# Layer norm chunks 1 to 7 turned one per step through the first product's bank, over twelve written-out steps, with the branch on the mask moved ahead

## The chip, the cores and the metric

The kernel runs on one core of one Trainium2 chip. The time is device microseconds (us) of one execution. Before the change three runs gave 430.34 us as median (429.97 to 431.79). The profiled execution took 429.76 us.

## The reference, cut to what matters

The input x has the shape (4, 32, 32, 128). Two blocks follow each other: a Swin block (layer norm, window attention with 16 heads of 8 channels in 64 windows of 64 tokens, projection, a gated MLP) and then a self-attention over 1024 tokens of each image. The change touches only the start of the first block:

```
xn = _layer_norm(x, norm1_g, norm1_b)            # over the 128 channels
xs = roll(xn, (-4, -4)); xw = windows of 8 x 8   # 64 windows, 64 tokens
qkv = xw @ qkv_w.T + qkv_b
q, k = rope2d(q), rope2d(k)
attn = softmax(q * scale @ k.T + attn_mask)      # attn_mask is 0 or -100
out = attn @ v
```

## The kernel before, in words

Five engines run instruction streams written by hand, and meet in semaphores: TensorE (PE), VectorE (DVE), ScalarE (ACT), GpSimd (POOL) and SyncE (SP), which issues transfers. Each works its own stream in order. The 4096 tokens lie in `x_all` as 32 pairs of windows, 128 tokens each. The layer norm takes four pairs at a time: 8 chunks of 512 tokens.

**A chunk of the layer norm** passes five stations: DVE takes the statistics (`ln_stats_of`, lines 800 and 804, four of each), POOL works out 1/sqrt(var + eps) and the shift (`ln_rstd_of`, lines 1041 to 1046), ACT scales the rows into `xn` (`ln_norm_of`, line 945, four instructions), PE transposes them into a PSUM bank (`ln_turn`, line 648, four f32 transposes), ACT copies the bank as its f16 high part (`ln_hi_of`), and DVE takes the rest as its f16 low part (`ln_lo_of`, line 819), which counts `ln_ready` up. Chunk 0 is done ahead of all steps.

**A step n** of the window attention, from -2 to 34, works on several pairs at once. PE's order in it is: the first product, q and k of pair n+2, into bank 4, `QKV_BANK` (lines 668 and 670); the first turn of pair n+1 (line 706, eight transposes, q and k); the scores of pair n (line 678, two mask products, then 687); the turned scores of pair n-1 (lines 678 and 699); the product with v of pair n-3 (line 761); the v product of pair n-1 (668, 670); the second turn of q of pair n (line 706, four transposes). Beside it DVE takes the two rope products from bank 4 (line 855), copies the first turn out (869), takes the low part of v (880), the row maxima of the scores (887) and writes them as two f16 columns (892, 894) that the second turn needs, and at last divides by the row sums (908, 912). ACT writes the q and k rows, the exponential (line 993), the copy of the second turn `q_t`, the high part of v, and the high part of the probabilities `p_hi` (those four from line 931 in the helper `copy`). POOL sums the rope (1064), takes the low part of the probabilities (1072) and those of q and k (1076, 1078). SP issues four transfers from `qk_t` to `k_t` (line 637), and the scores of a pair wait for them.

**Where the chunks stand before the change.** Chunks 1 and 2 are normed ahead of the steps and turned at the end of step -2 and in step -1. Chunks 3 and 4 are turned in step 0, 5 in step 1, 6 and 7 in step 2. They go through the banks of the turned scores and of the product with v (`LN_BANK`), which stand empty until step 3; `LN_BANK_FREE` tells which earlier chunk must be out. Steps -2 to 3 are written out, 4 to 27 are a loop of four steps with six passes, and 28 to 34 are written out.

**The branch on the mask.** PE has the steps from 0 on twice: with three bf16 parts of the mask and with one. The drawn mask needs one. PE reads the flag `mask_any` into a register in step -1, turns pair 0, waits for ACT's copy of the mask (`mask_hi`), and then branches.

Of the kernel before, what the change touches and what calls it, by code (L numbers as in the profile page):

```python
# [20 lines left out]
B, H, W, DIM = 4, 32, 32, 128  # L21
# [21 lines left out]
BUFS = 4  # L43
# [7 lines left out]
def build(nc, t):  # L51
    ctx = ExitStack()
    with ctx:
# [496 lines left out]
        with ExitStack() as st:  # L550
# [40 lines left out]
            def first_steps(body):  # L591
                for n in range(FIRST, 0):
                    body(n, n // 2, n % BUFS)

# [10 lines left out]
            def steps(eng, body, mlp_early):  # L605
                first_steps(body)
                other_steps(eng, body, mlp_early)

            def at_step(n, step):
                return isinstance(n, int) and n == step  # L610

            def valid(n, lag):
# [29 lines left out]
            def _(pe):  # L642
                def ln_turn(c):

                    pe.wait_ge(ln_norm, c + 1)
                    wait(pe, ln_ready, LN_BANK_FREE[c])
                    for k in range(TPC):
                        last = pe.transpose(ps[:, LN_BANK[c], 128 * k:128 * k + 128],
                                            xn[:, c % 4, 128 * k:128 * k + 128], ident[:])
                    last.then_inc(ln_turned, 1)  # L650
# [53 lines left out]
                def turn(out, rows):  # L704
# [3 lines left out]
                    return last  # L708

                def body(n, it, r, parts):  # L710
                    u = r % 2
                    v = 1 - u

                    if valid(n, -2):
                        wait(pe, rope_done, n + 2)

                        pe.wait_ge(ln_ready, (n + 2) // TPC + 1 if isinstance(n, int) and n < LOOP_FROM else CHUNKS)
                        project(qkv_ps[:, 0:2 * DIM], n + 2, slice(0, 2 * DIM)).then_inc(qk_done, 1)
                    if at_step(n, -2):

                        pe.wait_ge(mask_top, 1)
                        pe.matmul(ps[0:1, T1_BANK, 0:1], mask_max[:], ln_const[:, 2, 0:1], start=True,
                                  stop=True).then_inc(mask_summed, 1)
                    if at_step(n, -1):
                        ln_turn(2)

                        pe.wait_ge(mask_known, 1)
                        rest.append(pe.value_load(mask_any[0:1, 0:1].bitcast(mybir.dt.int32)))
                    if valid(n, -1):
# [4 lines left out]
                    if valid(n, 0):  # L734
# [3 lines left out]
                        scores(qk_t[:, u, 0], k_t[:, r], it, parts).then_inc(s_done, 1)  # L738
                    if at_step(n, 0):
                        ln_turn(3)  # L740
                        ln_turn(4)
                    if at_step(n, 1):

                        pe.wait_ge(ln_ready, 5)
                    if at_step(n, 2):
                        ln_turn(6)
                    if valid(n, 1):
# [3 lines left out]
                        scores_turned(k_t[:, (r - 1) % BUFS], q_t2[:, v], it if u else it - 1, parts).then_inc(st_done, 1)  # L751
                    if at_step(n, 1):
                        ln_turn(5)
                    if valid(n, 3):
                        wait(pe, plo_done, n - 2)
                        wait(pe, norm_done, n - 3)
                        pe.wait_ge(ln_ready, CHUNKS)
# [16 lines left out]

                    if at_step(n, -2):
                        ln_turn(1)
                    if at_step(n, 2):
                        ln_turn(7)

                rest = []  # L780
                first_steps(lambda n, it, r: body(n, it, r, 1))
                pe.wait_ge(mask_hi, 1)
                with pe.If(rest[0] > 0):
                    pe.wait_ge(mask_lo, 1)
                    other_steps(pe, lambda n, it, r: body(n, it, r, 3), mlp_pe(pe)[1])
                with pe.If(rest[0] < 1):
                    other_steps(pe, lambda n, it, r: body(n, it, r, 1), mlp_pe(pe)[1])

            @block.vector
            def _(dve):  # L790
# [25 lines left out]
                def ln_lo_of(c):  # L816

                    dve.wait_ge(ln_hi, c + 1)
                    dve.tensor_tensor(xn_all[:, TPC * c:TPC * c + TPC, 1, :],
                                      ps[:, LN_BANK[c], :].rearrange("p (t q) -> p t q", t=TPC),  # L820
                                      xn_all[:, TPC * c:TPC * c + TPC, 0, :], ALU.subtract).then_inc(ln_ready, 1)
# [24 lines left out]
                def body(n, it, r):  # L846
# [14 lines left out]
                    if at_step(n, -1):  # L861
                        ln_lo_of(1)
                        ln_stats_of(3)
                    if at_step(n, 3):
                        ln_lo_of(7)
                    if valid(n, -1):
# [3 lines left out]
                    if at_step(n, -1):  # L870
                        ln_lo_of(2)
                        ln_stats_of(4)
                        ln_stats_of(5)
                        ln_stats_of(6)
                    if valid(n, 2):
# [8 lines left out]
                    if valid(n, 0):  # L884
# [10 lines left out]
                                                 op0=ALU.mult, op1=ALU.subtract).then_inc(mlo_done, 1)  # L895
                    if at_step(n, 0):
                        ln_lo_of(3)
                        ln_lo_of(4)
                        ln_stats_of(7)
                    if at_step(n, 1):  # L900
                        ln_lo_of(5)
                    if at_step(n, 2):
                        ln_lo_of(6)
                    if valid(n, 3):
# [16 lines left out]
            def _(act):  # L921
# [11 lines left out]
                def ln_hi_of(c):  # L933

                    act.wait_ge(ln_turned, c + 1)
                    copy(xn_all[:, TPC * c:TPC * c + TPC, 0, :],
                         ps[:, LN_BANK[c], :].rearrange("p (t q) -> p t q", t=TPC)).then_inc(ln_hi, 1)

# [19 lines left out]
                ln_hi_of(0)  # L958
                ln_norm_of(1)
                ln_norm_of(2)  # L960
                ln_hi_of(1)

                def body(n, it, r):
# [10 lines left out]
                    if at_step(n, -1):  # L974
                        act.wait_ge(mask_loaded, 16)
                        copy(mask16[:, 0], mask_f[:]).then_inc(mask_hi, 1)
                        ln_norm_of(3)
                        ln_norm_of(4)

# [3 lines left out]
                        copy(proj_w16[:, 0, :], proj_ws[:]).then_inc(proj_w_hi, 1)  # L983
                    if at_step(n, 0):
                        ln_hi_of(3)
                        ln_hi_of(4)
                    if at_step(n, 2):
                        ln_hi_of(6)
                    if valid(n, 1):
# [4 lines left out]
                                       ACT.Exp).then_inc(exp_done, 1)  # L994
                    if at_step(n, 1):
                        ln_hi_of(5)
                        ln_norm_of(6)
                    if valid(n, 0):
# [3 lines left out]
                    if valid(n, 1):  # L1002
# [9 lines left out]
                        copy(p_hi[:, v], e_buf[:, v]).then_inc(phi_done, 1)  # L1012
                    if at_step(n, -2):
                        ln_hi_of(2)
                    if at_step(n, 0):
                        ln_norm_of(5)
                    if at_step(n, 1):
                        ln_norm_of(7)
                    if at_step(n, 2):
                        ln_hi_of(7)  # L1020

# [3 lines left out]
            def _(pool):  # L1025
# [31 lines left out]
                def body(n, it, r):  # L1057
# [22 lines left out]
                    if at_step(n, -1):  # L1080
                        ln_rstd_of(3)
                        ln_rstd_of(4)

                        pool.wait_ge(mask_known, 1)
                        with pool.If(pool.value_load(mask_any[0:1, 0:1].bitcast(mybir.dt.int32)) > 0):
# [12 lines left out]
                                .then_inc(mask_lo, 1)  # L1098
                    if at_step(n, 0):
                        ln_rstd_of(5)  # L1100
                        ln_rstd_of(6)
                    if at_step(n, 1):
                        ln_rstd_of(7)

                        pool.wait_ge(proj_w_hi, 1)
# [591 lines left out]
```

## Time and profile before

| what | value |
|---|---|
| median of three runs | 430.34 us (429.97 to 431.79) |
| the profiled execution | 429.76 us, its span 428.0 us |
| busy in the span: PE, DVE, ACT, POOL | 369.4, 306.4, 261.3, 231.6 us |
| of the chain that ended last: PE, DVE, ACT, issue | 59%, 19%, 9%, 5% |
| mean granted TensorE clock | 0.956 |

A busy time is the sum of an engine's instructions; the chain that ended last follows from the last instruction back through what released each one. In it "issue" is time in which the engine waited for nothing that the profile shows. Times are counted from the start of the span.

### The profile page before, as it was taken

How to read it: one execution, taken by the hardware profiler on the slowest of the kernel's cores; microseconds unless marked ns; L12 is line 12 of the kernel's file. 1: busy time of each engine (PE TensorE's matmuls, PEld its weight loads, DVE VectorE, ACT ScalarE, POOL GpSimd, SP SyncE). 2: the span in 40 equal slices, each digit the busy share in tenths (PEclk: the TensorE clock that was granted, in tenths of full speed). 3: DMA queues.
4: the chain of work that ended last, by engine and by line, in shares of the span. 5: the costliest groups of instructions: out<-in, count | busy, mean ns of one | idle time of the engine just before them, and what ended most of it. 6: DMA issues, size and time to landing. Idle time of an engine off the chain costs nothing.

```text
span 428.0 us, 12372 instructions
## 1 busy us (share of the span) xinstructions
PE 369.4 (86%) x4708; PEld 230.2 (54%) x4708; DVE 306.4 (72%) x850; ACT 261.3 (61%) x409; POOL 231.6 (54%) x288
## 2 busy tenths in 40 slices
PE   2567899999999999993999999999449998989794
PEld 0234555656566566572455555554215776767563
DVE  8767788888888888876465655553789787784524
ACT  2768777778777878692434333333407867768572
POOL 6656476777787777767253223310004774857511
PEclk9999999999999999996799999999957999999889
DMA  6701010110001100100000000000100102010101
GB/s 192 252 23 28 14 32 24 31 28 25 25 28 28 30 25 26 32 9 2 0 3 0 2 0 1 2 0 2 51 0 0 26 3 76 2 51 2 41 11 50
DMA packets 15580, 12.52 MB, mean 29 GB/s; under 512 B 3991, under 2 KB 14136, under 8 KB 15416
## 3 DMA queue, kind: packets, MB, share of 16 engines
q1 hardware_dynamic: 14144, 11.42, 9.2%
q10 hardware_dynamic: 1400, 0.61, 0.5%
q8 instruction: 24, 0.39, 0.4%
q14 instruction: 12, 0.10, 0.1%
HBM read 4.68 MB, written 2.10 MB: 16 GB/s over the span
## 4 chain that ended last, share of the span: by engine, by line
PE 59%; DVE 19%; ACT 9%; issue 5%; POOL 4%; DMA 2%; SPq 1%; DVEq 0%; POOLq 0%; ACTq 0%
PE ps L306 8%; PE ps L1324 7%; PE ps L314 6%; PE ps L678 5%; PE ps L706 5%; DVE mx L1460 4%; PE ps L668 3%; PE ps L761 3%; PE ps L1268 3%; PE ps L699 3%; PE ps L687 3%; DVE ob L1498 2%; DVE ps L887 2%; PE ps L670 2%; PE ps L1307 2%
## 5 line engine op out<-in xcount | busy, mean ns | idle before, releaser
L1586 POOL TENSOR_TENSOR el<-e,eh 128x1024 f16<-128x1024 f32 x28 | 59.6, 2132 | 77.7 <-ACT eh L1578 77.5
L1072 POOL TENSOR_TENSOR p_lo<-e_buf,p_hi 128x1024 f16<-128x1024 f32 x32 | 68.3, 2135 | 5.0 <-ACT p_hi L931 3.7
L1571 ACT ACTIVATE e<-ps 128x1024 f32<-128x1024 f32 x32 | 32.7, 1022 | 38.9 <-PE ps L1313 38.5
L306 PE MATMUL ps<-y_t,fc_w 128*128 128x512 f16 x192 | 47.7, 393 | 0.0
L1460 DVE TENSOR_REDUCE mx<-ps 128x1 f32<-128x1024 f32 x32 | 39.0, 1219 | 9.8 <-PE ps L1297 9.4
L1064 POOL TENSOR_TENSOR rot<-ta,tb 128x256 f32<-128x256 f32 x32 | 23.3, 729 | 40.5 <-DVE tb L855 40.4
L1324 PE MATMUL ps<-val,eh 128*128 128x129 f16 x512 | 38.3, 225 | 6.1 <-DVE ob L1498 5.3
L887 DVE TENSOR_REDUCE ps<-ps 128x16 f32<-128x1024 f32 x32 | 39.4, 1232 | 3.1 <-PE ps L687 2.2
L993 ACT ACTIVATE e_buf<-ps 128x1024 f32<-128x1024 f32 x32 | 32.8, 1024 | 14.4 <-PE ps L699 14.3
L678 PE MATMUL ps<-mask,identb 128*128 (+1 forms) x128 | 39.0, 386 | 2.6 <-DMA k_t<-qk_t 2.4
L1324 PEld LDWEIGHTS ps<-val,eh 128*128 128x128 f16 x512 | 32.8, 100 | 14.8 <-issue 8.8
L493 ACT ACTIVATE sg<-ps,fc_bias 128x512 f32<-128x512 f32 x32 | 22.0, 688 | 29.6 <-PE ps L306 26.6
L668 PE MATMUL ps<-qkv_w,xn_all 128*128 128x128 f16 (+1 forms) x192 | 27.4, 252 | 9.3 <-issue 7.7
L314 PE MATMUL ps<-hid,fc_ws 128*128 128x512 f32 x64 | 33.9, 611 | 0.8 <-POOL al L252 0.7
L931 ACT ACTIVATE p_hi<-e_buf 128x1024 f16<-128x1024 f32 x32 | 33.8, 1057 | 0.8
L403 DVE SCALAR_TENSOR_TENSOR hid<-ps,fc_bias,sg 128x512 f32<-128x512 f32 x32 | 24.0, 749 | 14.4 <-ACT sg L493 13.4
L1578 ACT ACTIVATE eh<-e 128x1024 f16<-128x1024 f32 x32 | 33.7, 1054 | 0.7
L306 PEld LDWEIGHTS ps<-y_t,fc_w 128*128 128x128 f16 x192 | 19.1, 101 | 27.8 <-issue 9.3
L706 PE MATMUL ps<-ident,q_rows 128*128 128x128 f16 x256 | 25.8, 224 | 5.0 <-DVE q_rows L894 3.2
L931 ACT ACTIVATE q_t<-ps 128x512 f16<-128x512 f16 x32 | 19.1, 597 | 12.7 <-PE ps L706 12.7
L699 PEld LDWEIGHTS ps<-q_t,k_t 128*64 128x64 f16 x1024 | 18.7, 112 | 13.6 <-issue 13.6
L761 PE MATMUL ps<-v_hi,p_hi 128*128 128x36 f16 x256 | 23.0, 180 | 2.0 <-POOL p_lo L1072 1.9
(148 smaller groups left out, 919.9 us busy)
## 6 DMA issues: line engine op xcount, KB each, us to landing
k_t<-qk_t SPq DMA_DIRECT2D x128, 32.0 KB, 1.8
x_all<-in_x SPq DMA_DIRECT2D x8, 256.0 KB, 5.8
out<-ob SPq DMA_DIRECT2D x8, 192.0 KB, 2.1
mask_f<-in_mask SPq DMA_DIRECT2D x1, 1024.0 KB, 4.8
yr<-xr SPq DMA_DIRECT2D x14, 64.0 KB, 2.0
fc_w<-in_fc_w SPq DMA_DIRECT2D x1, 512.0 KB, 7.1
out<-ob SPq DMA_DIRECT2D x4, 128.0 KB, 1.8
fc_w<-in_fc_w SPq DMA_DIRECT2D x1, 256.0 KB, 6.9
```

The costliest lines, as they stand in the source:

```text
L306: last = pe.matmul(ps[:, bank, :], fc1_w16[:, ws, 128 * block_:128 * block_ + 128], y_t[:, v, ys, :], start=(n == 0), stop=(n == 2))
L314: pe.matmul(ps[:, OUT_BANK, :], fc2_ws[:, k, :], hid[:, k % 2, :], start=(k == 0), stop=False, skip_group_check=True).then_inc(h_used, 1)
L668: pe.matmul(out, xn_all[:, at(i, 1), xs, :].rearrange("p a q -> p (a q)"), qkv_w16[:, ws, cols], start=(n == 0), stop=False, skip_group_ch ...
L678: pe.matmul(ps[:, bank + b, :].rearrange("p (h k) -> p h k", h=8), identb[:], mm, start=(part == 0), stop=False, skip_group_check=True)
L706: last = pe.transpose(out[:, c, :], rows[:, 4 * c:4 * c + 4, :].rearrange("p h r -> p (h r)"), ident16[:])
L761: last = pe.matmul(out, p[:, v, 2 * hp:2 * hp + 2, :].rearrange("p h q -> p (h q)"), w[:, v, hp].rearrange("p e r d -> p (e r d)"), start= ...
L887: dve.tensor_reduce(mx_ps, ps[:, S_BANK:S_BANK + 2, :].rearrange("p b (h k) -> p (b h) k", h=8), AX.X, ALU.max).then_inc(max_done, 1)
L931: return act.activation(out, in_, ACT.Copy)
L1072: pool.tensor_tensor(p_lo[:, u], e_buf[:, u], p_hi[:, u], ALU.subtract).then_inc(plo_done, 1)
L1324: return pe.matmul(pv4[:, j, i, 0:DIM + 1], weights[:, T % H_BUFS, 128 * n:128 * n + 128], val[:, b % 2, part, m, 0:DIM + 1], start=first, ...
L1460: dve.tensor_reduce(mx[:, k:k + 1], two(s_bank(k)), AX.X, ALU.max, negate=True).then_inc(max4_done, 1)
L1586: pool.tensor_tensor(el[:, T % H_BUFS, :], e4[:, T % E_BUFS, :], eh[:, T % H_BUFS, :], ALU.subtract).then_inc(el_done, 1)
```

## The change

Bank 4 now serves all chunks. Steps -2 to 11 are written out, and the loop runs from 12 to 27 in four passes. Chunks 1, 2, 3, 4, 5, 6, 7 are turned in steps 0, 2, 4, 6, 8, 10, 11, each after the scores of that step and ahead of the turned scores. ACT norms a chunk at the end of its step before (chunk 1 in step -1), copies its high part ahead of the exponential; DVE takes the low part after the maxima. The next first product waits for it, as it needs the same bank. The statistics of chunks 3 and 4 stay in step -1, now behind the copy of the first turn, and those of 5, 6, 7 go to steps 1, 3, 5; POOL's part of 3 to 7 goes to steps 1, 3, 5, 7, 9. PE issues the two first products of steps -2 and -1 next to each other, reads the flag, branches, and does the first turn of pair 0 and the wait for the mask's copy behind the branch.

```diff
-            LOOP_FROM, LOOP_TO = 4, PAIRS - 4
-            LN_BANK = (PV_BANK, ST_BANK, ST_BANK + 1, PV_BANK, ST_BANK, PV_BANK, PV_BANK, PV_BANK)
-            LN_BANK_FREE = (0, 0, 0, 1, 2, 4, 6, 7)
+            LOOP_FROM, LOOP_TO = 12, PAIRS - 4
+            LN_STEP = {0: 1, 2: 2, 4: 3, 6: 4, 8: 5, 10: 6, 11: 7}
...
+                def first_product(n):
+                    wait(pe, rope_done, n + 2)
+                    wait(pe, ln_ready, max([1] + [c + 1 for k, c in LN_STEP.items() if k < n])
+                         if isinstance(n, int) else CHUNKS)
+                    project(qkv_ps[:, 0:2 * DIM], n + 2, slice(0, 2 * DIM)).then_inc(qk_done, 1)
...
-                    if at_step(n, 0):
-                        ln_turn(3)
-                        ln_turn(4)
-                    if at_step(n, 1):
-                        pe.wait_ge(ln_ready, 5)
-                    if at_step(n, 2):
-                        ln_turn(6)
+                    if ln_chunk(n):
+                        pe.wait_ge(rope_done, n + 3)
+                        ln_turn(ln_chunk(n))
...
+                first_product(-2)
+                pe.wait_ge(mask_top, 1)
+                pe.matmul(ps[0:1, T1_BANK, 0:1], mask_max[:], ln_const[:, 2, 0:1], ...)
+                first_product(-1)
+                pe.wait_ge(mask_known, 1)
+                rest = pe.value_load(mask_any[0:1, 0:1].bitcast(mybir.dt.int32))
+                def steps_of(parts):
+                    part = lambda n, it, r: body(n, it, r, parts)
+                    part(-1, -1, BUFS - 1)
+                    pe.wait_ge(mask_lo if parts > 1 else mask_hi, 1)
+                    other_steps(pe, part, mlp_pe(pe)[1])
+                with pe.If(rest > 0):
+                    steps_of(3)
+                with pe.If(rest < 1):
+                    steps_of(1)
...   (DVE, after the maxima)
+                    if ln_chunk(n):
+                        ln_lo_of(ln_chunk(n))
+                    for c, step in ((5, 1), (6, 3), (7, 5)):
+                        if at_step(n, step):
+                            ln_stats_of(c)
...   (ACT, ahead of the exponential, and at the end of the step)
+                    if ln_chunk(n):
+                        ln_hi_of(ln_chunk(n))
...
+                    if isinstance(n, int) and n != -1 and ln_chunk(n + 1):
+                        ln_norm_of(ln_chunk(n + 1))
...   (POOL, at the end of the step)
+                    for c, step in ((3, 1), (4, 3), (5, 5), (6, 7), (7, 9)):
+                        if at_step(n, step):
+                            ln_rstd_of(c)
```

## Rows read from the trace of the kernel before

**Rows 1.** Windows: start:end length, then busy (count) per engine, PEclk, DMA share, GB/s.
```profile
14.00:18.00 4.00, 3.46 (x19) 2.07 (x17) 2.58 (x13) 2.75 (x8) 2.32 (x5) 1.00 1.06 371
37.58:44.99 7.41, 5.19 (x72) 3.35 (x73) 3.93 (x10) 7.31 (x17) 3.92 (x6) 1.00 0.07 20
50.23:70.97 20.74, 19.36 (x353) 12.05 (x353) 17.32 (x44) 15.47 (x29) 14.70 (x20) 1.00 0.11 29
70.97:90.53 19.56, 19.14 (x353) 12.05 (x353) 17.13 (x46) 15.76 (x29) 14.56 (x20) 1.00 0.09 26
```

**Rows 2.** Chain that ended last, 15 to 30 us: start, length, what.
```profile
18.59 1.81 ACT mask L931
20.40 4.13 issue
```

**Rows 3.** Timeline of PE around the branch: start, length, instruction, [idle before <-releaser].
```profile
14.26 0.85 PE L668 MATMUL ps<-qkv_w,xn_all 128*128 128x256 f16 x3
17.02 0.61 PE L706 MATMUL ps<-ident,q_rows 128*128 128x128 f16 x4 [0.54 <-POOL k_rows L1078]
24.53 0.80 PE L668 MATMUL ps<-qkv_w,xn_all 128*128 128x256 f16 x3 [6.48 <-issue]
26.42 1.06 PE L678 MATMUL ps<-mask,identb 128*128 128x512 bf16 x2
28.40 1.09 PE L648 MATMUL ps<-ident,xn 128*128 128x128 f32 x8
30.33 0.40 PE L706 MATMUL ps<-ident,q_rows 128*128 128x128 f16 x4 [0.83 <-DVE q_rows L894]
30.56 0.49 PE L668 MATMUL ps<-qkv_w,xn_all 128*128 128x256 f16 x3
```

**Rows 4.** Timeline of PE, first products of steps 2, 3, 4; turn of chunk 7.
```profile
35.80 0.49 PE L668 MATMUL ps<-qkv_w,xn_all 128*128 128x256 f16 x3
...
43.44 0.63 PE L648 MATMUL ps<-ident,xn 128*128 128x128 f32 x4 [1.85 <-DVE xn_all L819]
43.90 0.49 PE L668 MATMUL ps<-qkv_w,xn_all 128*128 128x256 f16 x3
...
50.23 0.50 PE L668 MATMUL ps<-qkv_w,xn_all 128*128 128x256 f16 x3
```

**Rows 5.** Timeline of PE, one loop step and the loop's back edge.
```profile
104.95 0.50 PE L668 MATMUL ps<-qkv_w,xn_all 128*128 128x256 f16 x3
...
107.13 0.61 PE L678 MATMUL ps<-mask,identb 128*128 x2
...
109.40 0.40 PE L706 MATMUL ps<-ident,q_rows 128*128 128x128 f16 x4
110.13 0.28 PE L668 MATMUL ps<-qkv_w,xn_all 128*128 128x256 f16 x1 [0.33 <-issue]
```

**Rows 6.** Timeline of ACT: norm of chunk 7, then the same loop step.
```profile
39.70 1.63 ACT L945 ACTIVATE xn<-x_all,nmr,rstd 128x128 f32<-128x128 f32 x4
...
105.08 0.60 ACT L931 ACTIVATE q_t<-ps 128x512 f16<-128x512 f16 x1 [0.37 <-PE ps L706]
...
106.19 1.06 ACT L931 ACTIVATE p_hi<-e_buf 128x1024 f16<-128x1024 f32 x1
```

**Rows 7.** Timeline of DVE: statistics, a low part, maxima of the loop step.
```profile
31.33 0.86 DVE L800 BATCH_NORM_STATS2 stats<-x_all 128x6 f32<-128x128 f32 x4
...
42.60 0.69 DVE L819 TENSOR_TENSOR xn_all<-ps,xn_all 128x512 f16<-128x512 f32 x1 [1.47 <-ACT xn_all L931]
...
107.59 1.23 DVE L887 TENSOR_REDUCE ps<-ps 128x16 f32<-128x1024 f32 x1
```

**Rows 8.** Chain that ended last, 50 to 57 us: copy, transfer, scores.
```profile
51.76 0.69 DVE qk_t L869
...
54.69 1.84 DMA k_t<-qk_t
56.58 0.60 PE ps L678 x2
```

More of the change, by code:

```diff
@@ L582, in build @@
             FIRST, LAST = -2, PAIRS + 2
-            LOOP_FROM, LOOP_TO = 4, PAIRS - 4
-            LN_BANK = (PV_BANK, ST_BANK, ST_BANK + 1, PV_BANK, ST_BANK, PV_BANK, PV_BANK, PV_BANK)
-            LN_BANK_FREE = (0, 0, 0, 1, 2, 4, 6, 7)
+            LOOP_FROM, LOOP_TO = 12, PAIRS - 4
+            LN_STEP = {0: 1, 2: 2, 4: 3, 6: 4, 8: 5, 10: 6, 11: 7}
             def nothing(left):
                 pass
-            def first_steps(body):
-                for n in range(FIRST, 0):
-                    body(n, n // 2, n % BUFS)
             def other_steps(eng, body, mlp_early):
@@ L605, in steps @@
             def steps(eng, body, mlp_early):
-                first_steps(body)
+                for n in range(FIRST, 0):
+                    body(n, n // 2, n % BUFS)
                 other_steps(eng, body, mlp_early)
@@ L610, in at_step, with ln_chunk @@
                 return isinstance(n, int) and n == step
+            def ln_chunk(n):
+                return LN_STEP.get(n) if isinstance(n, int) else None
             def valid(n, lag):
@@ L645, in ln_turn @@
                     pe.wait_ge(ln_norm, c + 1)
-                    wait(pe, ln_ready, LN_BANK_FREE[c])
                     for k in range(TPC):
-                        last = pe.transpose(ps[:, LN_BANK[c], 128 * k:128 * k + 128],
+                        last = pe.transpose(ps[:, QKV_BANK, 128 * k:128 * k + 128],
                                             xn[:, c % 4, 128 * k:128 * k + 128], ident[:])
@@ L712, in body @@
                     v = 1 - u
[L714 to L728, printed above, removed]
+                    if valid(n, -2) and not at_step(n, -1):
+                        first_product(n)
                     if valid(n, -1):
@@ L756, in body @@
                         wait(pe, norm_done, n - 3)
-                        pe.wait_ge(ln_ready, CHUNKS)
                         for hp in range(HP):
@@ L773, in body @@
                         turn(t2_ps, q_rows[:, r]).then_inc(t2_done, 1)
[L775 to L787, printed above, removed]
+                first_product(-2)
+                pe.wait_ge(mask_top, 1)
+                pe.matmul(ps[0:1, T1_BANK, 0:1], mask_max[:], ln_const[:, 2, 0:1], start=True,
+                          stop=True).then_inc(mask_summed, 1)
+                first_product(-1)
[10 more added lines that the diff above has]
+                    steps_of(1)
             @block.vector
@@ L819, in ln_lo_of @@
                     dve.tensor_tensor(xn_all[:, TPC * c:TPC * c + TPC, 1, :],
-                                      ps[:, LN_BANK[c], :].rearrange("p (t q) -> p t q", t=TPC),
+                                      ps[:, QKV_BANK, :].rearrange("p (t q) -> p t q", t=TPC),
                                       xn_all[:, TPC * c:TPC * c + TPC, 0, :], ALU.subtract).then_inc(ln_ready, 1)
@@ L860, in body @@
                         dve.tensor_copy(mask_any[0:1, :], ps[0:1, T1_BANK, 0:1]).then_inc(mask_known, 1)
[L861 to L865, printed above, removed]
                     if valid(n, -1):
@@ L870, in body @@
                     if at_step(n, -1):
-                        ln_lo_of(2)
+                        ln_stats_of(3)
                         ln_stats_of(4)
-                        ln_stats_of(5)
-                        ln_stats_of(6)
                     if valid(n, 2):
@@ L936, in ln_hi_of @@
                     copy(xn_all[:, TPC * c:TPC * c + TPC, 0, :],
-                         ps[:, LN_BANK[c], :].rearrange("p (t q) -> p t q", t=TPC)).then_inc(ln_hi, 1)
+                         ps[:, QKV_BANK, :].rearrange("p (t q) -> p t q", t=TPC)).then_inc(ln_hi, 1)
                 def ln_norm_of(c):
@@ L958, in _ @@
                 ln_hi_of(0)
-                ln_norm_of(1)
-                ln_norm_of(2)
-                ln_hi_of(1)
                 def body(n, it, r):
@@ L976, in body @@
                         copy(mask16[:, 0], mask_f[:]).then_inc(mask_hi, 1)
-                        ln_norm_of(3)
-                        ln_norm_of(4)
+                        ln_norm_of(1)
                         act.wait_ge(attn_loaded, 16 * len(ATTN))
@@ L1080, in body @@
                     if at_step(n, -1):
-                        ln_rstd_of(3)
-                        ln_rstd_of(4)
                         pool.wait_ge(mask_known, 1)
@@ L1098, in body @@
                                 .then_inc(mask_lo, 1)
[L1099 to L1103, printed above, removed]
+                    for c, step in ((3, 1), (4, 3), (5, 5), (6, 7), (7, 9)):
+                        if at_step(n, step):
+                            ln_rstd_of(c)
+                    if at_step(n, 2):
                         pool.wait_ge(proj_w_hi, 1)
```

26 lines of the change are left out of this document (removed).

## The prediction

> **What bounds the kernel now.** I first read the chain of waits over the span, then the windows by stage, then the timelines of the engines next to each other. From step 4 on PE sets the pace: in one pass of the loop it is busy 19.14 of 19.56 us, DVE 17.13, ACT 15.76, POOL 14.56 [rows 1]. The back edge adds 0.33 us [rows 5]; without it a step takes (19.56 - 0.33) / 4, about 4.80 us, from first product to first product. Whatever is added to PE's stream there lengthens the kernel, and a wait in it cannot be won back, since PE has only 0.4 us of idle time per pass. Before step 4 it is otherwise. PE waits 6.48 us in front of the first product of step 0 [rows 3], of which the chain gives 1.81 us to ACT's copy of the mask and 4.13 us to issue, behind the branch [rows 2]; and steps 0 to 3 take from 24.53 to 50.23 us [rows 3, 4], 25.7 us where four steps at 4.80 would be 19.2. Step 2 shows why: ACT is busy 7.31 of 7.41 us [rows 1], and PE waits 1.85 us for the bank of chunk 7 [rows 4].
>
> So the change trades: it can gain in the 26 us of steps 0 to 3 and at the branch, and it pays in steps 4 to 11, where PE has nothing to give.
>
> **The branch.** Both first products ahead of it end by 15.1 (before, the second started at 14.26 and took 1.2 [rows 3]). The 4.13 us of issue [rows 2] then end at 19.2, beside ACT's copy of the mask, which ends by about 20.0. The first turn of pair 0, which stood at 17.02 and waited for POOL [rows 3], moves to 19.2 and takes 1.0 (half of it is the row of 0.61). Its copy on DVE ends at 20.95. The transfer chain from the end of that copy to the scores was 52.45 to 56.58, 4.1 us [rows 8], so the scores of step 0 start at 25.05. Before, they started at 26.42 [rows 3]. Between the two, PE does the first product of step 0 and the first turn of pair 1, off the path. The branch is worth 1.4 us and no more, because the transfer follows the moved turn. Its price in the worst case: at 14 to 18 us the DMA engines are fully taken, share 1.06 [rows 1], while before the branch they were quiet. If what the branch waits for must come behind these loads, it ends at 18.0 + 4.13 = 22.1, and the front is 3 us later than I sum. The trace has no branch under such load; I take 4.13, the only row.
>
> **Steps 0 and 1.** The turn of chunk 1 follows the scores (2.0 us from 26.42 to 28.40 [rows 3]; here to 27.05), the maxima and their columns take 1.8 us on DVE to 28.85, the low part 0.69 [rows 7], so the product of step 1 starts at 29.5 where it was 30.56 [rows 3]. A second effect takes that back. Up to 28.4 matmuls take about twice their later time: four turns 0.61 us at 17.02 and 0.40 at 30.33 [rows 3], though the granted clock reads 1.00, the full level of 2.4 GHz, throughout [rows 1]. They became fast after PE had worked without a gap from 24.53. After the change PE stops at about 22.3, at 25.05 and at 27.9 again, so I take step 1 as slow up to the end of its scores: product and turn 1.9 (24.53 to 26.42 [rows 3]) and scores 2.0 give 33.4, maxima and their columns 1.8, second turn 0.35. The product of step 2 starts at 35.6, against 35.80 [rows 4]. Fast from 29.5 on, it would start at 34.0. Those are the two bounds, 1.6 us apart.
>
> **A step with a chunk.** This is the term that decides. PE's turn of chunk c stands behind the scores of step n. Its input is ACT's norm, four instructions, 1.63 us [rows 6], at the end of ACT's step n-1. ACT comes to that end late: `q_t` waits for PE's second turn of step n-1 and starts at 105.08, when PE already begins step n (104.95 [rows 5]); the high part of v and `p_hi` follow, to 106.19 + 1.06 = 107.25 [rows 6]. In the loop PE is through the scores at 107.13 [rows 5]. With the norm behind `p_hi`, PE's turn can start at 107.25 + 1.63 and some 0.09 of hand-over = 108.97, about 1.8 us after PE gets there. Behind it all of PE's queue waits: turned scores, product with v, v product, second turn. ACT's idle time in this step does not help, as it lies at the exponential and the second turn, both fed by PE. The turn itself is 0.46 to 0.49 us (43.44 to 43.90 [rows 4]). Together 2.25 us for each chunk. From below: the turn alone, 0.49, if the norm were in time. From above: 2.25 plus a late low part. That one I cost at nothing: ACT writes the high part within 1.3 us of the turn, DVE is through its maxima (109.4 - 107.1 = 2.3 us behind the scores [rows 5, 7]) long before PE is through the step, the low part takes 0.69 [rows 7], and PE needs 2.6 us from the turned scores to the next product. If that cover went, the low part would cost up to 0.7 per chunk.
>
> Steps 4, 6, 8, 10, 11 have a chunk: 5 x 2.25 = 11.25. The eight steps take 8 x 4.80 + 11.25 = 49.65 us. Before, they took 20.74 + 19.56 = 40.30 [rows 1]. Loss: 9.35 us.
>
> **Steps 2 and 3.** The product of step 2 is at 35.6, `p_hi` ends 2.2 us later at 37.8, the norm at 39.45, chunk 2 is turned to 40.0, and the turned scores, v product and second turn (1.9 us, no product with v yet) give the product of step 3 at 41.9, before 43.90. Step 3 has no chunk: 41.9 + 4.80 = 46.7 for step 4, before 50.23 [rows 4]. Gain at this point: 3.5 us, the branch's 1.4 within it.
>
> **Cost at nothing.** Statistics, 1.24 us on DVE (0.86 [rows 7] and the four aggregates) in steps 1, 3, 5: they push the next rope, but the next step is one with a chunk, in which PE stands still 1.8 us anyway; in a step without that cover each would cost up to 1.2. POOL's 1.6 us per chunk in the odd steps lie under the same stall. The writes of q and k rows, now behind the norm, are needed a step later. On SP nothing is added; a copy of the first turn that is 1.2 us later still leaves more than the 4.1 us of its chain.
>
> **The loop.** Two passes fewer take away two back edges; my 4.80 per step leaves both out already. The entry at step 12 still pays 0.3. The first pass of before is 1.2 us longer than the second [rows 1]; I don't know whether this goes, stays or moves to step 12, and keep 0 to 1.2 for the range.
>
> Sum: -3.5 + 9.35 + 0.3 = +6.15 us. The profiled execution would be 429.76 + 6.15 = 435.9; the median shown is 0.58 above it, so 436.5 us.
>
> On branches the trace holds two kinds: 4.13 us of issue behind the one on the mask [rows 2], 0.33 at a back edge of the loop [rows 5]. The Trainium skill (Runtime: NRT & Kernel Launch, Instruction fetch mechanics) says that a taken branch to a target outside the two fetched pages must wait for a DMA fetch, and that kernels prefer unrolling for this. It speaks for this change, since a pass of four steps of PE has over 700 matmuls and weight loads [rows 1] and by that rule each of the two back edges removed would be worth a fetch. The first kind of row agrees with it, the second does not.
>
> **The rivals.**
> (1) Norm in time. If ACT got to the norm before PE was through the scores, a chunk would cost 0.49 in place of 2.25: 5 x 0.49 = 2.45 in steps 4 to 11, loss 0.55, and step 2 1.8 us shorter, gain at the front 5.3. Then -5.3 + 0.55 + 0.3 = -4.5, 425.9 us: faster. For it: ACT has 3.8 us idle per pass. Against: it lies behind PE's second turn, and `p_hi` ends at 107.25 against PE's 107.13. It decides where the stall per chunk falls below 0.6 us. Half a stall, 0.9 us, gives about +0.7: no change.
> (2) The branch under load ends at 22.1: +3.0 on the forecast, 439.5 us. For it: the share of 1.06. Against: the fetch is small beside the loads.
> (3) Back edges dear. If each were worth 4.13, two fewer would turn +6.15 into -1.5, 428.8 us. Against: every back edge's row has about 0.3.
> (4) DVE becomes the bound: steps with statistics or a low part add 0.7 to 1.2 each beyond the forecast, in some four of them: +3, 439.5 us. For it: 17.13 of 19.56 busy [rows 1]. Against: the chunk steps are long.
> (5) The steps are ordered otherwise than I read and the turn waits elsewhere; about the size of (1)'s half, 431 us.
>
> **Chances.** Forecast 0.62; (1) 0.09, half of it 0.06; (2) 0.09; (3) 0.02; (4) 0.07; (5) 0.05. Own range of the forecast: stall 1.2 to 2.0 per chunk over six steps, clock 1.6, first pass 1.2, so 432 to 439.5. With rivals (2) and (4) and part of the halves: 431.0 to 441.0. A measurement of this kernel tells a change from none at about 0.5%, 2.15 us: slower beyond that 0.78, within it 0.11, faster 0.11.
>
> **What would show it.** In the changed kernel, each turn on line 648 in steps 4, 6, 8, 10, 11 should stand behind an idle time of PE of about 1.8 us released by ACT's norm; steps with a chunk should take 7.05 us, the others 4.8. The branch's issue should lie between 15 and 19.2 and the scores of step 0 at 25.05; the product of step 12 should come near 96.7 us, 6.15 behind its 90.53. The prediction is wrong if the turn waits less than 0.6 us, if a step with a chunk takes under 5.8 us, or if the front gains over 6 us.

## The result, and the profile after

The changed kernel takes 438.03 us (median of 4 executions, 437.2 to 439.08), the kernel before beside it 431.06. The ratio is 1.0164, 95% interval 1.0124 to 1.0204: slower by 7.0 us, where 6.15 were forecast. The profiled execution has a span of 437.2 us, 9.2 more than the 428.0 of before.

Where the time is lost, by the starts of the first product in PE's timeline of both kernels:

| first product of step | before | predicted | after | after - before |
|---|---|---|---|---|
| 0 | 24.53 | (20.2) | 21.69 | -2.84 |
| 1 | 30.56 | 29.5 | 31.10 | +0.54 |
| 2 | 35.80 | 35.6 | 36.68 | +0.88 |
| 3 | 43.90 | 41.9 | 43.01 | -0.89 |
| 4 | 50.23 | 46.7 | 47.69 | -2.54 |
| 12 | 90.53 | 96.7 | 96.40 | +5.87 |
| 16 | 110.13 | | 117.52 | +7.39 |
| 28 | 168.29 | | 175.83 | +7.54 |
| end of span | 428.0 | | 437.2 | +9.2 |

The windows of the changed kernel (start:end and length; busy time and count of PE, PEld, DVE, ACT, POOL; PEclk; DMA share; GB/s) show the same by stage. They answer to [rows 1]:

```profile
47.69:96.40 48.71, 40.11 (x727) 26.42 (x725) 40.23 (x110) 41.05 (x81) 36.27 (x60) 1.00 0.09 25
96.40:117.52 21.12, 19.26 (x355) 12.04 (x353) 17.46 (x45) 15.45 (x29) 14.72 (x20) 1.00 0.10 28
117.52:137.09 19.57, 19.11 (x352) 12.04 (x353) 17.19 (x46) 15.81 (x29) 14.60 (x20) 1.00 0.09 25
175.83:437.00 261.17, 228.36 (x2303) 142.39 (x2302) 167.64 (x466) 136.27 (x174) 112.83 (x102) 0.91 0.06 15
```

In steps 4 to 11 PE is busy 40.11 of 48.71 us; before, it was busy 38.50 of 40.30 us there [rows 1]. The first pass of the loop takes 21.12 us and the next 19.57. At step 28 the changed kernel is 7.5 us behind. From there to the end 261.4 us pass, before 259.7: the same instructions, with a granted clock of 0.91 where this window of before has 0.93. One stretch at half clock in it has no counterpart before:

```profile
388.90:392.30 3.40, 3.40 (x27) 2.10 (x25) 2.14 (x6) 1.39 (x2) 1.21 (x1) 0.50 0.17 47
```

That last 1.7 us is no part of the change's mechanism as far as I can show; with it the two spans differ by 9.2 us. The medians, over all executions, differ by 7.0.

PE's waits over the whole span of the changed kernel (engine, line <- releaser: us in total, times, longest) name the cause:

```profile
PE ps L647 <- ACT xn L927: 8.8, 6, 1.8
PE ps L677 <- DMA k_t<-qk_t: 6.3, 7, 2.7
PE ps L705 <- issue: 5.6, 1, 5.6
```

The first line is the turn of a chunk waiting for ACT's norm, six times; before, no turn in the steps waited for a norm. The second is the scores waiting for a transfer to `k_t`, before five times and 2.4 us. The third is the branch, with the reading of the flag ahead of it. One of the six, in PE's timeline of step 11:

```profile
93.51 0.63 PE L647 MATMUL ps<-ident,xn 128*128 128x128 f32 x4 [1.80 <-ACT xn L927]
```

The chain that ended last, in step 11 of the changed kernel (start, us, what), has the first wait in full; it answers to [rows 5, 6]:

```profile
90.77 1.06 ACT p_hi L913
91.83 1.55 ACT xn L927 x4
93.51 0.63 PE ps L647 x4
94.14 0.43 PE ps L677 x2
94.57 0.62 PE ps L698 x32
95.20 0.70 PE ps L746 x24
```

The chain leaves PE, which should own it in these steps, and goes through ACT's `p_hi` and the four norm instructions back to PE's turn. And PE's timeline around the branch (start, us, instruction, [idle before <-releaser]), answering to [rows 3]:

```profile
14.09 0.82 PE L667 MATMUL ps<-qkv_w,xn_all 128*128 128x256 f16 x3 [0.81 <-DVE tb L847]
20.87 0.60 PE L705 MATMUL ps<-ident,q_rows 128*128 128x128 f16 x4 [5.64 <-issue]
26.52 1.04 PE L677 MATMUL ps<-mask,identb 128*128 128x512 bf16 x2 [2.69 <-DMA k_t<-qk_t]
```

The branch went some 5 us earlier (its issue starts at 15.2 and not at 20.40), and the issue grew from 4.13 to 5.64 us; the 5.64 also hold the reading of the flag, which stood earlier before. The scores of step 0 start at 26.52 where they started at 26.42: the moved branch bought nothing there.

### The profile page after: what moved, and what is told of

It reads as the page before. It is cut to its first block, busy times and chain, and to the rows that moved or that the text cites. A ratio compares the mean times of both kernels' runs of the same rounds, so it can differ in the third digit from the quotient of the medians.

```text
span 437.2 us, 12232 instructions
## 1 busy us (share of the span) xinstructions
PE 371.2 (85%) x4708; PEld 231.3 (53%) x4708; DVE 307.2 (70%) x850; ACT 261.0 (60%) x409; POOL 231.5 (53%) x288
## 3 DMA queue, kind: packets, MB, share of 16 engines
HBM read 4.68 MB, written 2.10 MB: 15 GB/s over the span
## 4 chain that ended last, share of the span: by engine, by line
PE 60%; DVE 17%; ACT 10%; issue 5%; POOL 3%; DMA 3%; SPq 2%; DVEq 0%; POOLq 0%; ACTq 0%
PE ps L1286 7%; PE ps L306 7%; PE ps L314 6%; PE ps L677 5%; PE ps L705 5%; DVE mx L1422 4%; PE ps L746 4%; PE ps L698 3%; PE ps L667 3%; PE ps L1230 3%; PE ps L686 3%; ACT p_hi L913 2%; ACT xn L927 2%; DMA k_t<-qk_t 2%; DVE ob L1460 2%
## 5 line engine op out<-in xcount | busy, mean ns | idle before, releaser
L306 PE MATMUL ps<-y_t,fc_w 128*128 128x512 f16 x192 | 46.7, 387 | 0.0
L677 PE MATMUL ps<-mask,identb 128*128 128x512 bf16 (+1 forms) x128 | 39.3, 390 | 6.3 <-DMA k_t<-qk_t 6.3
L856 DVE COPY qk_t<-ps 128x1024 f16<-128x1024 f16 x32 | 21.9, 683 | 7.1 <-PE ps L705 7.1
```

The source lines that it names most:

```text
L306: last = pe.matmul(ps[:, bank, :], fc1_w16[:, ws, 128 * block_:128 * block_ + 128], y_t[:, v, ys, :], start=(n == 0), stop=(n == 2))
L677: pe.matmul(ps[:, bank + b, :].rearrange("p (h k) -> p h k", h=8), identb[:], mm, start=(part == 0), stop=False, skip_group_check=True)
```

## The experiments

**Norm ahead of the exponential** (norm_early). The changed kernel, with ACT's four norm instructions moved within ACT's step; nothing else.

```diff
+                    if isinstance(n, int) and n != -1 and ln_chunk(n + 1):
+                        ln_norm_of(ln_chunk(n + 1))
                     if valid(n, 1):
                         act.wait_ge(st_done, n)
...
-                    if isinstance(n, int) and n != -1 and ln_chunk(n + 1):
-                        ln_norm_of(ln_chunk(n + 1))
```

> The changed kernel with ACT's norm of a chunk moved within its step, from behind the high part of the probabilities to ahead of the exponential. Theory (the turn waits for the norm, 1.75 us in each of six steps): the idle time of PE before the turns of chunks 2 to 7 goes to under 0.3 us each, the steps with a chunk take 5.3 us in place of 6.93; ACT gives 0.3 to 1.0 us of it back in the step ahead, whose exponential comes later; in all 5 to 9 us faster than the changed kernel, ratio to before 0.995 to 1.005. Rival (ACT is at its limit, the stall only moves): less than 3 us faster than the changed kernel, ratio above 1.009.

Measured: 432.11 us, ratio 1.0037 (1.0010 to 1.0064), 5.5 us less than the changed kernel by the ratios. PE's waits from 20 to 125 us of it:

```profile
PE ps L677 <- DMA k_t<-qk_t: 6.0, 8, 2.7
PE ps L705 <- issue: 5.9, 1, 5.9
PE ps L705 <- DVE q_rows L879: 1.1, 2, 0.8
PE ps L667 <- DVE xn_all L811: 0.8, 3, 0.3
PE ps L705 <- POOL k_rows L1044: 0.6, 2, 0.3
```

The wait for the norm is gone, not smaller, and step 12 starts at 88.89, 7.5 us earlier than in the changed kernel and 1.6 earlier than in the kernel before. The steps with a chunk take 5.98, 6.00, 5.08, 5.33 and 5.84 us (6.93 in the changed kernel); ACT gives little back. The stall was one of place, not of ACT's capacity. Not all of the 7.5 us is the norm: step 1 alone takes 4.33 us and not 5.58, as its matmuls are fast earlier. And the profiled execution (428.63 us) is one of the fastest of eleven, so the medians give 5.5 us.

**The turn later in PE's stream** (turn_late, turn_late_hi). The other end of the same wait: leave the norm where it is, and let PE do its other work first.

```diff
-                    if ln_chunk(n):                 # PE, ahead of the turned scores
-                        pe.wait_ge(rope_done, n + 3)
-                        ln_turn(ln_chunk(n))
...                                                  # PE, behind the product with v
+                    if ln_chunk(n):
+                        pe.wait_ge(rope_done, n + 3)
+                        ln_turn(ln_chunk(n))
...                                                  # ACT, turn_late only: behind the exponential
+                    if ln_chunk(n):
+                        ln_hi_of(ln_chunk(n))
```

> The changed kernel with PE's turn of a chunk moved within its step, from ahead of the turned scores to behind the product with v, and ACT's copy of it from ahead of the exponential to behind it. The norm stays at the end of ACT's step before. Theory (all that counts is what stands in PE's queue behind the wait for the norm): PE does 1.8 us of other work first, the idle time before the turn goes to 0.1 us; the low part comes too late for the next product by 0.3 to 0.6 us; a chunk costs 1.0 us in place of 2.25, 6 to 8 us faster than the changed kernel in all. Rival (DVE or ACT sets the step with a chunk): these steps stay above 6.3 us, less than 3 us faster.

Measured: 442.79 us, ratio 1.0248 (1.0187 to 1.0310). The expectation failed: slower even than the change. The turn no longer waits (but for 0.79 us in step 2), but the next first product does. PE and then ACT in one step with a chunk:

```profile
77.23 0.63 PE L647 MATMUL ps<-ident,xn 128*128 128x128 f32 x4
80.10 0.80 PE L667 MATMUL ps<-qkv_w,xn_all 128*128 128x256 f16 x3 [1.59 <-DVE xn_all L811]
```

```profile
75.45 1.64 ACT L927 ACTIVATE xn<-x_all,nmr,rstd 128x128 f32<-128x128 f32 x4
76.99 0.40 ACT L913 ACTIVATE q_rows<-rot 128x256 f16<-128x256 f32 x1
77.29 0.40 ACT L913 ACTIVATE k_rows<-rot 128x256 f16<-128x256 f32 x1
77.72 1.02 ACT L966 ACTIVATE e_buf<-ps 128x1024 f32<-128x1024 f32 x1
78.64 0.59 ACT L913 ACTIVATE xn_all<-ps 128x512 f16<-128x512 f32 x1
```

I had let the exponential run before the turn was done. The norm pushes it back to 77.72, so the high part (78.64) stands behind it, then DVE's low part, and bank 4 comes free 2.9 us after the turn began. The step takes 6.92 us, as in the change. What makes turn_late slower than the change is mostly something else: steps 1, 2, 3, 9 and 11 take 6.07, 7.07, 5.86, 6.06 and 7.71 us and not 5.58, 6.33, 4.68, 4.69 and 6.93, and in three of them the granted clock fell to 0.50, the lower of its two levels, for a stretch (here step 9; the others from 45.9 and 93.7 us):

```profile
80.00:83.40 3.40, 3.30 (x18) 1.73 (x20) 2.61 (x8) 1.80 (x4) 1.30 (x2) 0.50 0.03 7
```

turn_late_hi puts the high part back ahead of the exponential:

> turn_late with ACT's high part of the chunk back ahead of the exponential. In turn_late PE waited 1.6 us per chunk for the low part, since the high part stood behind an exponential that the norm had pushed back. If that is all of turn_late's failure: the wait for the low part falls to 0.6 us, the steps with a chunk take 5.9 us in place of 6.93, five to six of them, so 5 to 6 us faster than the changed kernel, ratio 1.002 to 1.006. If not: these steps stay at 6.9 and the ratio above 1.014.

Measured: 436.66 us, ratio 1.0150 (1.0109 to 1.0191). Steps 8, 10 and 11 take 6.18, 6.17 and 6.20 us, PE waits 0.85 to 0.95 us for the low part behind each, and step 12 starts at 92.59, 8.2 us earlier than in turn_late and 3.8 earlier than in the change. Steps 4 and 6 take 7.18 and 6.49 us, since the scores wait 0.91 and 0.22 us for `k_t` in them as well. The order on ACT was worth about 0.75 us per chunk (steps 8 and 10). Of the 8.2 us, 4.3 lie in steps 1, 3 and 9, which the slow matmuls of turn_late made long, so they say nothing of the order. What is left to wait for is the chain turn, high part, low part, bank free: about 2 us in series, which needs work of PE behind the turn. The ratio missed the expected 1.002 to 1.006. Its median is above what the trace lets one expect, and its interval overlaps that of the change; by the ratio alone this one is unclear.

**Only more steps written out** (unroll_only, unroll_20). The kernel before with one number changed, 4 to 12 or to 20.

```diff
-            LOOP_FROM, LOOP_TO = 4, PAIRS - 4
+            LOOP_FROM, LOOP_TO = 12, PAIRS - 4
```

> The kernel before with one edit: the loop starts at step 12, so steps 4 to 11 are written out; all chunks stay where they were. Theory (the chunks' waits for ACT's norm make the change slow, and the slow first pass belongs to the entry into the loop): within 1 us of before; written-out steps of 4.8 us, then a first pass of the loop from step 12 of about 21 us where before it took 19.6. Rival (written-out code itself is slow, and carries part of the 7 us): slower by 2 us or more, steps 4 to 11 above 5.0 us each.

> The kernel before with the loop from step 20, 16 more steps written out in place of unroll_only's 8; chunks and branch as before. Theory (fetched blocks of instructions delay transfers to k_t, so that scores wait; each written-out step pays on the average): the waits of the scores for k_t are spread over steps 4 to 23, the loss to before is larger than unroll_only's 3.0 us, 4 to 6 us, ratio 1.010 to 1.014. Rival (the loss comes once, at the entry of the loop): the same 3 us, ratio 1.007.

Measured: unroll_only 432.83 us, ratio 1.0070 (1.0046 to 1.0094); unroll_20 435.91 us, 1.0130 (1.0069 to 1.0190). Both are slower, by 3.0 and 5.6 us, as the rival for the first and the theory for the second had it. The two intervals overlap, so the medians alone don't show that twice as many steps cost twice as much. The steps of the traces say where the time goes, and for unroll_only they say something else than its rival. At step 28 it is 4.2 us behind the kernel before: 1.8 of this is there at the start of step 4, lost in steps 2 and 3, which are written out in both kernels, 1.1 come in step 4, and 1.6 in the first pass of the loop from step 12, which takes 21.2 us as the theory had it. Steps 5 to 11 take 35.1 us, before 35.3. In step 2 the scores waited 2.43 us for a transfer to `k_t` that landed after 3.7 us, and the granted clock (third from the end in this window's row) stood at half, here and once more from 51.8 to 55.2 us:

```profile
38.10:44.90 6.80, 5.72 (x55) 3.16 (x56) 2.88 (x6) 4.86 (x10) 3.09 (x5) 0.50 0.07 19
```

unroll_20 is 3.8 us behind at step 28, of which 2.7 in the written-out steps 4 to 19 and 0.9 in the first pass of the loop: about 0.2 us for each of the 16 steps. In it PE waits for `k_t` ten times, 8.3 us, eight of them in steps 5 to 22. The views of transfers show with what they coincide. The loop of before (71 to 168 us), then 50 to 110 us of unroll_20 (queue, kind: packets, MB, share):

```profile
q1 hardware_dynamic: 3744, 2.56, 9.6%
q14 instruction: 1, 0.01, 0.0%
```

```profile
q1 hardware_dynamic: 2281, 1.56, 9.5%
q8 instruction: 8, 0.13, 1.0%
q14 instruction: 3, 0.02, 0.1%
```

The loop fetches one block of instructions in 97 us, the written-out steps eleven in 60. The 80 transfers to `k_t` that are issued between 70 and 168 us of the kernel before take 1.8 to 1.9 us from issue to landing. While blocks are fetched, single ones take up to 3.7 us. In the changed kernel, for 100 to 105 and 110 to 115 us:

```profile
DMA to landing us min/median/max: 1.9/2.4/2.9
DMA to landing us min/median/max: 1.8/1.8/3.5
```

Laid over the times of the instruction packets in the same traces, every transfer to `k_t` of more than 2.2 us has such a packet under way: 15 of 15 in the kernel before, 10 of 10 in the change, 21 of 21 in unroll_only, 22 of 22 in unroll_20. Of the shorter ones 5 of 113, 14 of 118, 13 of 107 and 19 of 106 have one. The slow first pass of the loop, before (50 to 71 us) and after (96 to 118 us), has its packets too.

The scores of a pair wait for the slowest of four transfers and have about 4 us for copy, issue and landing, so a landing of 3 us shows at once on PE. That the blocks cause the late landings is inferred from this coincidence, in time and in number; no run held the blocks back with the code unchanged. The Trainium skill (Runtime: NRT & Kernel Launch, Instruction fetch mechanics) says that an engine's instructions are refilled in blocks of 16 KiB, by a DMA queue that the sequencer drives. The profile of the changed kernel agrees for q8, 29 packets with 0.48 MB; the 13 of q14 hold 0.11 MB, about half as much each. The same section of the Trainium skill says that kernels prefer full unrolling where possible, and that the cost of crossing a block is mostly hidden. Here it was not, beside transfers that have no time to spare, and the measurement decides: 3.0 us for eight steps and 5.6 us for 16.

**The branch** (branch_only, branch_back, loads_late, before_loads, branch_loads). branch_only moves the branch alone in the kernel before; branch_back takes it alone out of the change.

```diff
                 first_product(-1)
+                ln_turn(2)                                    # branch_only
...
+                body(-1, -1, BUFS - 1, 1)                     # branch_back: ahead of the branch,
+                pe.wait_ge(mask_hi, 1)                        # as in the kernel before
```

> The kernel before with the branch alone moved: both first products and the turn of chunk 2 ahead of it, then the branch, the first turn of pair 0 and the wait for the mask's copy behind it. Chunks stay where they were. Theory: the scores of step 0 start where they do after the change (26.5 us, held by the transfer that follows the moved turn) or a little before, against 26.42; so the branch is worth nothing, 0 to 1 us either way. Rival (the branch brought a gain that the chunks ate): faster by 1.5 us or more.

> The changed kernel with the branch where it stood before, behind the first turn of pair 0 and the wait for the mask's copy; chunks as in the change. Theory (the moved branch is worth nothing in the change, as the turn it holds back starts at 20.87 in place of 17): the first turn starts at 16.6 us, its transfers land by 22.5, the branch's issue ends at 24.2 to 24.6, scores of step 0 at 26.2; within 0.7 us of the changed kernel, ratio to before 1.014 to 1.018. Rival (it was worth the 1.4 us of the prediction): 1.4 us slower than the changed kernel, ratio 1.019 or more.

Measured: branch_only 434.63 us, ratio 1.0111 (1.0077 to 1.0145), a loss; branch_back 436.31 us, 1.0143 (1.0091 to 1.0196), not slower than the change. In branch_only the issue takes 5.0 us, and then the transfer for step 0 lands only after 3.35 us, so the scores of step 0 start at 28.80, 2.4 us behind before. In branch_back they start at 26.02, half a microsecond ahead of the change. The moved branch is worth nothing or less.

loads_late asks why the issue grew. It is the change with the nine loads of later weights moved out of the first 16 us.

```diff
-                for dst, name in REST:
-                    sp.dma_start(dst[:], t[name]).then_inc(rest_loaded, 16)
...   (SP, behind the four transfers of a step)
+                    # one load each in steps 1 to 9
+                    for dst, name in REST_OF_STEP.get(n, ()):
+                        sp.dma_start(dst[:], t[name]).then_inc(rest_loaded, 16)
```

> The changed kernel, with the nine loads of the MLP's and the second block's weights (1.2 MB) issued one per step in steps 1 to 9, behind the transfers of the step, in place of ahead of all steps. Theory (the moved branch waits behind these loads: 5.64 us of issue where it was 4.13 in the kernel before): the issue falls back to 4.1 us or less, the first turn starts at 18 to 19.5 us in place of 20.87, the scores of step 0 at 23.7 to 25.1, and the kernel is 1.4 to 2.9 us faster than the changed one, ratio to before 1.009 to 1.013. Rival (the branch's time has nothing to do with the loads): issue 5.6 us as it was, ratio 1.016 or more, as the loads now stand beside the transfers.

Measured: 436.79 us, ratio 1.0149 (1.0102 to 1.0196). PE around the branch:

```profile
18.58 0.60 PE L705 MATMUL ps<-ident,q_rows 128*128 128x128 f16 x4 [3.36 <-issue]
20.06 0.82 PE L667 MATMUL ps<-qkv_w,xn_all 128*128 128x256 f16 x3 [0.45 <-ACT mask L913]
24.29 1.03 PE L677 MATMUL ps<-mask,identb 128*128 128x512 bf16 x2 [2.11 <-DMA k_t<-qk_t]
```

The issue falls from 5.64 to 3.36 us and the scores of step 0 come 2.2 us earlier. So the branch is slower when it is taken beside the loads. The mean DMA share was 0.56 over the issue in the change and 0.06 here. Of the 2.2 us nothing is left at step 12 (97.40 against 96.40), and the median is above the expected 1.009 to 1.013. That the loads now stand beside the transfers explains little of this: the scores wait 0.46 us for `k_t` in step 7. Steps 3 and 11, 0.8 and 0.7 us longer than in the change, stand under a granted clock of 0.50 for part of their time, from 40.6 and from 95.2 us:

```profile
95.20:98.50 3.30, 3.30 (x58) 2.23 (x51) 1.47 (x4) 1.86 (x4) 0.07 (x1) 0.50 0.02 6
```

Two more of this kind:

> The kernel before with the nine loads issued in steps 0 to 3. Theory: its branch is taken at 20.4 us when the loads are over, so nothing is won: the product of step 0 stays at 24.5 us, ratio 0.998 to 1.004. Rival (loads delay other things in the first 20 us, the mask's copy or the chunks' rows among them): product of step 0 earlier by 0.5 us or more, ratio below 0.998.

> branch_only (chunks where they were before the change, branch moved) with the nine weight loads behind the transfers of steps -1 and 0. Theory: the branch costs 5 us of issue in branch_only because it waits beside the loads; without them it ends by 19.5 us, the scores of step 0 start at 23.8 to 25, 1.5 to 2.5 us ahead of the kernel before, and nothing is paid for chunks: ratio 0.993 to 0.997. Rival (a block of instructions that is fetched when the transfer of step 0 is on its way delays it by 1.5 us, as in branch_only, where it took 3.35): scores of step 0 at 25.5 to 26.5, ratio 0.998 to 1.003.

before_loads, with the loads in steps 0 to 3 of the kernel before: 429.61 us, ratio 0.9985 (0.9960 to 1.0010), product of step 0 at 24.39. As expected: without the early branch the loads cost nothing. branch_loads, branch moved and loads behind the transfers of steps -1 and 0, chunks as before: 431.10 us, ratio 1.0032 (1.0009 to 1.0055). The theory fell, and its rival held as far as its numbers go. Its chain:

```profile
16.96 2.35 issue
19.31 1.04 PE ps L706 x8
20.38 0.70 DVE qk_t L874
23.08 3.04 DMA k_t<-qk_t
26.17 1.03 PE ps L678 x2
```

The turn starts at 19.31, but the transfer lands after 3.04 us, and PE's matmuls are then still slow (the eight f32 transposes of chunks 3 and 4 take 1.91 us, before 1.09 [rows 3]). The product of step 4 starts at 50.28, before at 50.23.

**Both remedies together** (norm_loads, loads_front): norm_early with the loads in steps 1 to 9, or behind the transfers of steps -1 and 0.

> norm_early (norm ahead of the exponential) with the same nine loads in steps 1 to 9. Both theories together: norm_early's 1.0037 less 1.4 to 2.9 us, ratio 0.997 to 1.000, the first version at or below before. If the loads only move the trouble: ratio 1.003 or more.

> norm_early with the nine weight loads behind the transfers of steps -1 (five of them) and 0 (four). Theory: the early branch is kept (first turn at 18.6, scores of step 0 at 24.3), and the loads no longer stand beside the transfers of steps 1 to 9; 1 to 2 us faster than norm_loads, ratio to before 0.991 to 0.995. Rival (they now delay the transfers of step 0, needed by the scores of step 1): ratio 0.996 or more.

Measured: norm_loads 428.56 us, ratio 0.9967 (0.9938 to 0.9995); loads_front 428.58 us, 0.9973 (0.9952 to 0.9994). Both are about 0.3% below the kernel before, 1.2 to 1.4 us, and beat both kernels of this case. loads_front does not gain the further 1 to 2 us that I expected. In the steps it does: its step 12 starts at 86.61, 1.2 us ahead of norm_loads (87.83), and at step 28 it is still 1.0 ahead (165.55 against 166.54). The profiled execution loses this behind step 28 (261.6 us to the end against 260.1), with 46.9 us at half clock and not 40.6.

## Why the prediction was right, and where it was off

- **A chunk costs 2.25 us in steps that PE bounds.** Shown. The five steps with a chunk take 6.94, 6.93, 6.93, 6.93 and 6.93 us and the others 4.7; the turn waits 1.65 to 1.8 us in all but step 4. There the scores waited 1.14 us for `k_t` first, and only 0.20 was left for the norm. The eight steps take 48.71 us where 49.65 were worked out. The cause, ACT's order, is what norm_early takes away. The loop's entry, for which 0.3 us were added, shows no wait: step 11 takes 6.93 us like the others.
- **The front.** The branch was mis-sized: I took 4.13 us for it beside full DMA engines, and it took 5.64, the reading of the flag included, which I had put at nothing. This was rival (2), at half its size, and loads_late shows its mechanism. The scores of step 0 came at 26.52 and not 25.05. Behind that the sum runs true: steps 1 to 4 are 1.6, 1.1, 1.1 and 1.0 us later than worked out. The stretch of slow matmuls ends inside step 1 (its product of q and k is fast, 0.63 us from 33.96), between the two bounds. "About twice" was too much: 1.5 times for the turns (0.61 and 0.40), 1.8 for the mask products (1.06 and 0.60). And the granted clock of 1.00 that I read there was no evidence: the first clock record of either trace starts where the matmuls turn fast, at 28.4 us before and 33.9 after, and a window without a record reads 1.00. Gain at step 4: 2.54 us, predicted 3.5.
- **At step 12** the errors nearly cancel, which is luck: a front that is 1.0 us worse, eight steps that are 0.9 us better, and an entry of 0.3 us that did not come: 96.40 against 96.7. With the next term the trace comes to 7.5 us at step 28, so a median of 7.0 against 6.15 looks closer than the terms were.
- **The loop's first pass.** The term that I left at zero, with 1.2 us as its bound, is 1.55 us: the slow first pass of before is found again at step 12, and by the coincidence above the reason is the fetched blocks. I priced written-out steps like loop steps; the row that spoke against it, 20.74 against 19.56 us [rows 1], I had read and not explained. In steps 4 to 11 of the change PE waits 1.1 us for `k_t`, in those of norm_early 1.7. That the longer steps of the change hide part of the price, since a transfer has more time to land in them, would fit this small difference and isn't shown.
- **Back edges dear (3)** is refuted: those that are left in the change show 0.29 to 0.36 us each. DVE as the bound (4): no wait of PE for DVE in steps 4 to 11 of the change. The turn waits where I had it, so (5) is out. Norm in time (1) did not happen; norm_early is what it would have looked like. It gives 1.0037 and not the 4.5 us of gain: at step 28 it stands at 168.00, before at 168.29. Steps 4 to 11 take 42.9 us and not 40.85, the first pass of the loop is 1.35 us longer than the second of before, and the front is 1.0 us worse than that rival had it.
- **Open.** Why the changed kernel's last 261 us had a lower granted clock than before's; why the clock fell inside the steps of some runs and not in those of the change, where PE stood still up to 1.8 us at a time; and why turn_late_hi's median is no better than its trace of the steps.

## What to carry to other kernels

When a step is added to a producer chain across engines, look at where in the feeding engine's order it stands, not at how much idle time that engine has: ACT had 0.9 us free per step and still held PE 1.7 us, and moving four instructions ahead of an instruction that waits for PE gave 5.5 us back. Writing out a loop was not free here, with transfers of little slack beside it; look at their landing times in both kinds of code. Before a difference is put down to an edit, compare step by step and read the granted clock of the steps that differ: in three runs of this case part of it was the clock. A branch moved earlier is only worth what the next wait behind it leaves, here nothing, as the transfer behind it moved too.

## What the runs showed of the hardware

- The branch on the mask cost PE 4.13 us of issue when taken at 20.40 us, with a DMA share of 0.11 (4.12 in branch_back). Taken at 15 to 17 us it cost 5.64 and 4.96 us with a share of 0.56 and 0.45, and 2.83 to 3.36 with the later loads out of the way. Why the late one costs more than the early one without loads is open. A loop's back edge cost 0.3.
- A 32 KB transfer between partitions lands in 1.8 to 1.9 us in the loop, over 97 us; with a packet of instructions under way single ones take 2.3 to 3.7 us.
- Four f16 transposes took 0.60 us at 20.87 and 0.40 at 36.45 in the changed kernel. The windows read a granted clock of 1.00 at both, but the trace has no clock record before 33.9 us.
- The granted clock fell to 0.50 inside the steps of seven runs. In unroll_only, turn_late and loads_late steps became longer by it; in unroll_20, branch_only, before_loads and branch_loads, once each at 44.5 to 46.3 us, no step by more than 0.3 us. In unroll_only PE stood still for 2.43 us up to 39.18, and the clock fell at 38.1; in turn_late for 1.59 us up to 80.10, and it fell at 80.0. In the change PE waited up to 1.80 us in its steps from 4 on, and the clock stayed at 1.00.
